# Sixteen-head attention on one core: diagonal blocks of four heads in one bank, output copies on ScalarE, the split of the maxima on GpSimd

## What is computed

```python
c_q = x @ W_dq
Q = (c_q @ W_uq).reshape(Bx, Sx, N_HEADS, D_K)      # 16 heads of 16
c_kv = x @ W_dkv
K = (c_kv @ W_uk).reshape(Bx, Sx, N_HEADS, D_K)
V = (c_kv @ W_uv).reshape(Bx, Sx, N_HEADS, D_K)
scores = jnp.einsum('bqhd,bkhd->bhqk', Q, K) / math.sqrt(D_K)
scores = jnp.where(causal, scores, -jnp.inf)
attn = jax.nn.softmax(scores, axis=-1)
out = jnp.einsum('bhqk,bkhd->bqhd', attn, V).reshape(Bx, Sx, N_HEADS * D_K)
return out @ W_o
```

## Time and profile before

| what | us |
|---|---|
| runs | 1255.91 median of 3 (1251.33 to 1259.59) |
| the profiled execution | 1263.3 span |
| attention steps in it | about 423 to 920 |
| engines over the span | TensorE 84%, VectorE 66%, ScalarE 53%, GpSimd 30% busy |

### The profile page before, as it was taken

The page is one execution under the profiler, slowest core; times in us unless marked ns, Lnnn a source line. Parts: engine busy times, 40 slices in busy tenths (PEclk is TensorE's granted clock), DMA queues, the critical chain, the costliest instruction groups (busy, mean ns, idle before and its releaser), DMA issues. The chain is left out here.

```text
span 1263.3 us, 22520 instructions
## 1 busy us (share of the span) xinstructions
PE 1066.7 (84%) x6988; PEld 642.3 (51%) x6988; DVE 829.9 (66%) x2536; ACT 666.1 (53%) x1668; POOL 384.3 (30%) x404
## 2 busy tenths in 40 slices
PE   3539999984988899999999999999859369999940
PEld 2328888872442244443444444444347258888840
DVE  6774444436867888888888888888037754444427
ACT  5605554542753376676777666667636315455520
POOL 6506777752002000000000000000048227777730
PEclk8559999995977699999999999999889759999985
DMA  9503333326756444444444444440057113333339
GB/s 301 186 9 93 101 105 105 102 84 216 201 200 142 59 60 61 61 61 60 61 61 60 60 61 61 61 60 11 10 189 239 58 38 94 104 102 104 105 118 331
DMA packets 109248, 132.53 MB, mean 105 GB/s; under 512 B 29968, under 2 KB 83664, under 8 KB 109136
## 3 DMA queue, kind: packets, MB, share of 16 engines
q1 hardware_dynamic: 91280, 89.65, 31.2%
q0 software_dynamic: 13632, 37.24, 9.3%
q10 hardware_dynamic: 4224, 4.19, 1.0%
HBM read 82.42 MB, written 48.23 MB: 103 GB/s over the span
## 5 line engine op out<-in xcount | busy, mean ns | idle before, releaser
L1415 ACT ACTIVATE stacks_rows_or_prob<-stacks_bank 128x512 f32<-128x512 f32 (+3 forms) x768 | 326.0, 494 | 144.1 <-PE stacks_bank L1347 118.9
L1429 DVE CUSTOM_DVE_ANT_0 stacks_bank<-stacks_bank,all_causal 128x128 f32<-128x128 f32 (+3 forms) x512 | 245.4, 504 | 33.7 <-PE stacks_bank L1318 30.2
L1432 DVE TENSOR_REDUCE t_maxp<-stacks_bank 128x1 f32<-128x512 f32 x256 | 175.5, 686 | 25.0 <-PE stacks_bank L1318 24.4
L1318 PE MATMUL stacks_bank<-stacks_kst,stacks_qst 96*128 96x512 bf16 (+2 forms) x528 | 160.3, 348 | 8.5 <-DVE t_maxp L1429 4.2
L1358 PE MATMUL stacks_bank<-stacks_rows_or_prob,stacks_turned_or_values 128*32 128x512 f32 (+3 forms) x1536 | 164.5, 500 | 3.0 <-ACT stacks_rows_or_prob L1415 1.1
L1344 PE MATMUL stacks_bank<-stacks_qst,stacks_kst 99*128 99x512 bf16 (+3 forms) x528 | 154.9, 335 | 2.5 <-ACT stacks_rows_or_prob L1415 1.9
L1296 POOL COPY stacks_turned_or_values<-stacks_values 128x512 f32<-128x512 f32 x16 | 9.8, 613 | 427.7 <-DMA stacks_kst<-qk_parts 286.5
L1318 PEld LDWEIGHTS stacks_bank<-stacks_kst,stacks_qst 96*128 96x128 bf16 x528 | 48.5, 98 | 126.9 <-DVE t_maxp L1429 66.6
L653 PE MATMUL be_psG<-b_w,be_xT 128*128 x426 | 112.8, 401 | 0.0
L653 PE MATMUL ae_psG<-a_w,ae_xT 128*128 x426 | 111.9, 398 | 0.0
L1347 PE MATMUL stacks_bank<-all_causal_t,all_ident_bf 128*128 128x128 bf16 x512 | 109.6, 221 | 0.0
(11 more groups left out here) (296 smaller groups left out, 1917.7 us busy)
## 6 DMA issues: line engine op xcount, KB each, us to landing
stacks_qst<-qk_parts SPq DMA_DIRECT2D x66, 128.0 KB, 4.9
stacks_kst<-qk_parts SPq DMA_DIRECT2D x66, 128.0 KB, 7.6
stacks_rows_or_prob<-y_rows SPq DMA_DIRECT2D x16, 512.0 KB, 6.1
s_yk<-y_rows SPq DMA_DIRECT2D x16, 512.0 KB, 9.4
stacks_parts_or_stacks<-qk_parts SPq DMA_DIRECT2D x60, 128.0 KB, 6.2
qk_parts<-stacks_parts_or_stacks SPq DMA_DIRECT2D x16, 384.0 KB, 2.6
qk_parts<-q_parts SPq DMA_DIRECT2D x16, 384.0 KB, 3.4
o_rows<-t_orow SPq DMA_DIRECT2D x32, 136.0 KB, 8.7
```

The lines of the kernel that those rows point to most:

```text
L1318: nc.tensor.matmul(psR[bank][:, 0:w], qst[slot][0:KROWS, h, i * P:(i + 1) * P], kst[slot][0:KROWS, h, k0:k0 + w], start=True, stop=True).t ...
L1415: nc.scalar.activation(prob[j % 2][:, h, a:(c + 1) * 512], psS[n % ST_BANKS][:, a - c * 512:512], ACT.Exp, scale=DK ** -0.5).then_inc(exp_ ...
L1429: ins = nc.vector.tensor_tensor_reduce(psR[bank][:, 0:w], psR[bank][:, 0:w], T.causal[:, 512 - w:512], 1.0, -BIG, ALU.add, ALU.max, maxp[: ...
L1432: ins = nc.vector.tensor_reduce(maxp[:, h, col:col + 1], psR[bank][:, 0:w], AX_X, ALU.max)
```

## The change

Three edits, all in the attention.

1. The turned scores of one key tile's diagonal block are taken out of the heads' units. For each j, one unit (j, c, None) of 4 x 128 columns holds the diagonal blocks of all four heads: one matmul with the mask repeated four times (512 columns) opens the bank, and four matmuls of 128 columns add the scores. The heads' own units are 128 columns narrower, and those of width 0 are gone. There are again 48 units. The planner knows the new units; its fixed cost of an exponential goes from 100 to 70 ns.
2. `copy_rows` moves from VectorE to ScalarE, behind the exponential that stands at the place of `turn_out` in the list. It has a semaphore of its own, `rows_copied`; who reuses that ring bank waits for it (`free_bank`).
3. Of `split_max`, negating stays on VectorE (`negate_max`); the other four instructions go to GpSimd. GpSimd's values copy is made two steps ahead, behind the split, where it was made in its own step.

The diff, cut to its core:

```diff
+def transposed_units():
+    units = []
+    for j in range(QT):
+        for c in range(j // QHALF, 2):
+            if c == j // QHALF:
+                units.append((j, c, None, HG * P))
+            w = (c + 1) * 512 - max(c * 512, (j + 1) * P)
+            units += [(j, c, h, w) for h in range(HG) if w > 0]
+    return units
...
-            _, j, c, h = st[n_st]
-            w = width(j, c)
-            t = start + (w + P * (max(c * 512, j * P) == j * P)) / 2.4
-            act = max(act, t + READER_LATENCY) + 100 + w * 0.833
+            j, c, h, w = st[n_st]
+            t = start + (w + (h is None) * w) / 2.4
+            act = max(act, t + READER_LATENCY) + 70 + w * 0.833
...
+        def split_max(g):
+            pool.wait_ge(drained, drained_to(max_at[g]))
+            wait(pool, m_loaded, g * (16 * PARTS))
+            nc.gpsimd.tensor_copy(mparts[:, 0], neg[:]).then_inc(split, 1)
+            pool.wait_ge(split, g * SPLIT + 1)
+            nc.gpsimd.tensor_tensor(mid[:], neg[:], mparts[:, 0], ALU.subtract).then_inc(split, 1)
+            pool.wait_ge(split, g * SPLIT + 2)
+            nc.gpsimd.tensor_copy(mparts[:, 1], mid[:]).then_inc(split, 1)
+            pool.wait_ge(split, g * SPLIT + 3)
+            nc.gpsimd.tensor_tensor(mparts[:, 2], mid[:], mparts[:, 1], ALU.subtract).then_inc(m_ready, 1)
+
+        def step(g, k, later, with_before):
+            if later:
+                split_max(g + 1)
+            if later > 1:
+                values_of(g + 2, (k + 2) % SLOTS)
...
-        def score_t(g, k, j, c, h):
-            n, a = n_st[j, c, h], max(c * 512, j * P)
-            ps = psS[n % ST_BANKS][:, a - c * 512:512]
-            wait(pe, exp_done, g * ST + n + 1 - ST_BANKS)
-            ins = nc.tensor.matmul(ps, kst[k][0:MROWS, h, j * P:(j + 1) * P], qst[k][0:MROWS, h, a:(c + 1) * 512],
-                                   start=True, stop=a > j * P)
-            if a == j * P:
-                ins = nc.tensor.matmul(ps[:, 0:P], T.ident_bf[:], T.causal_t[:], start=False, stop=True)
+        def score_t(g, k, n):
+            j, c, h, w = st_units[n]
+            ps, keys = psS[n % ST_BANKS], slice(j * P, (j + 1) * P)
+            wait(pe, st_read, g * ST + n + 1 - ST_BANKS)
+            if h is None:
+                nc.tensor.matmul(ps[:], T.ident_bf[:], bc(T.causal_t[:], 1, [P, HG, P]), start=True, stop=False)
+                for x in range(HG):
+                    ins = nc.tensor.matmul(ps[:, x * P:(x + 1) * P], kst[k][0:MROWS, x, keys], qst[k][0:MROWS, x, keys],
+                                           start=False, stop=(x == HG - 1))
+            else:
+                ins = nc.tensor.matmul(ps[:, 0:w], kst[k][0:MROWS, h, keys], qst[k][0:MROWS, h, (c + 1) * 512 - w:(c + 1) * 512],
+                                       start=True, stop=True)
             ins.then_inc(st_done, 1)
...
+        def copy_rows(g, c):
+            r = out_at(g, c) - 1
+            act.wait_ge(filled, r + 1)
+            wait(act, o_stored[c], g * 16)
+            nc.scalar.copy(orow[:, c], psR[r % RING_BANKS][:].rearrange("p (x w) -> p x w", w=VW)[:, :, 0:OW]).then_inc(rows_copied, 1)
...
+                if h is None:
+                    nc.scalar.activation(prob[j % 2][:, :, j * P:(j + 1) * P], psS[n % ST_BANKS][:].rearrange("p (h t) -> p h t", h=HG),
+                                         ACT.Exp, scale=DK ** -0.5).then_inc(st_read, 1)
...
+                for half in range(2):
+                    if n == turned[half]:
+                        copy_rows(g - 1, half)
...
-        def split_max(g, r, bank):
+        def negate_max(g, r, bank):
             dve.wait_ge(filled, r + 1)
-            wait(dve, m_loaded, g * (16 * PARTS))
+            wait(dve, m_ready, g)
             nc.vector.tensor_scalar(neg[:], psR[bank][0:MROW, 0:P], -1.0, None, ALU.mult).then_inc(drained, 1)
-            dve.wait_ge(drained, r + 1)
-            link(nc.vector.tensor_copy(mparts[:, 0], neg[:]), g, 2)
-            link(nc.vector.tensor_tensor(mid[:], neg[:], mparts[:, 0], ALU.subtract), g, 3)
-            link(nc.vector.tensor_copy(mparts[:, 1], mid[:]), g, 4)
-            nc.vector.tensor_tensor(mparts[:, 2], mid[:], mparts[:, 1], ALU.subtract).then_inc(m_ready, 1)
-
-        def copy_rows(g, c, r, bank):
-            dve.wait_ge(filled, r + 1)
-            wait(dve, o_stored[c], g * 16)
-            nc.vector.tensor_copy(orow[:, c], psR[bank][:].rearrange("p (x w) -> p x w", w=VW)[:, :, 0:OW]).then_inc(drained, 1)
```

More of the change, by code:

```diff
@@ L54 @@
 QT = S // P
+QHALF = QT // 2
 BIG = 3.0e38
@@ L1118, in score_units, with parts_of @@
     return units
+def transposed_units():
[7 more added lines that the diff above has]
+    return units
+def parts_of(units, j, c):
+    return [unit[:3] for unit in units if unit[:2] == (j, c)]
 def plan_step(units, later, with_before):
     width = lambda j, c: min((c + 1) * 512, S) - max(c * 512, j * P)
+    st = transposed_units()
     ring = [("s", u, 1) for u in range(AHEAD, len(units))] if later else []
@@ L1152, in plan_step @@
             _, j, c = pv[n_pv]
-            ready = max(exp_end.get((j, c, h), float("inf")) for h in range(HG))
+            ready = max(exp_end.get(key, float("inf")) for key in parts_of(st, j, c))
             can.append((max(t, ready), 0.0, "p"))
@@ L1175, in plan_step @@
             had_t += w
-            order.append(st[n_st])
+            order.append(("st", n_st))
             n_st += 1
@@ L1196, in programs_attention @@
     NS = len(units)
-    QHALF = QT // 2
     MROW = HG * QT
     n_pv = {(j, c): n for n, (j, c) in enumerate((j, c) for j in range(QT) for c in range(2) if j < QHALF * (c + 1))}
-    n_st = {(j, c, h): n * HG + h for (j, c), n in n_pv.items() for h in range(HG)}
+    st_units = transposed_units()
+    n_st = {unit[:3]: n for n, unit in enumerate(st_units)}
     PV, ST = len(n_pv), len(n_st)
@@ L1213, in programs_attention @@
     o_stored = [M.sem(f"o_stored{c}") for c in range(2)]
[L1214 to L1216 removed]
+    m_loaded, filled, drained, rows_copied, max_ready, m_ready, st_done, st_read, pv_done, o_copied, \
+        pool_done, joined, split = (
+            M.sem(n) for n in ("m_loaded", "filled", "drained", "rows_copied", "max_ready", "m_ready", "st_done", "st_read",
+                               "pv_done", "o_copied", "pool_done", "joined", "split"))
     RING0 = NS + 1 + AHEAD
@@ L1224, in programs_attention, with drained_to, free_bank @@
     assert RING % RING_BANKS == 0 and ST % ST_BANKS == 0
+    kinds = ["s"] * NS + ["m"] + ["s"] * AHEAD
+    for g in range(NG):
+        kinds += [x[0] for x in plans[min(2, NG - 1 - g), g > 0][1]]
+    kinds += ["o"] * 2
+    max_at = [r for r, kind in enumerate(kinds) if kind == "m"]
+    copied_by_act = list(itertools.accumulate(kind == "o" for kind in kinds))
+    def drained_to(r):
+        return r + 1 - copied_by_act[r]
+    def free_bank(pe, r):
+        before = r - RING_BANKS
+        if before >= 0 and kinds[before] == "o":
+            pe.wait_ge(rows_copied, copied_by_act[before])
+        elif before >= 0:
+            pe.wait_ge(drained, drained_to(before))
     def steps(step):
@@ L1290, in gpsimd, with values_of @@
         first = Q.pool_chain
-        def step(g, k, later, with_before):
+        def values_of(g, k):
             wait(pool, loaded[k], ((g - k) // SLOTS) * (16 * N_LOADS) + 16 * N_LOADS)
@@ L1297, in step @@
                                              rows.rearrange("p j (h w) -> p j h w", w=DK)))
-            if g == 0:
-                for s in range(1, SLOTS):
-                    blank(s)
-                pool.wait_ge(Q.v_ready, 2 * Q.CH)
-                for stored in Q.parts_stored:
-                    pool.wait_ge(stored, (Q.CH // 2) * (16 * Q.NU))
-                first.link(nc.gpsimd.memset(kst[SLOTS - 1][KROWS:MROWS, :, :], 1.0))
         def blank(s):
@@ L1312, in gpsimd @@
         pool.wait_ge(Q.v_ready, Q.CH)
+        values_of(0, 0)
+        for s in range(1, SLOTS):
+            blank(s)
+        pool.wait_ge(Q.v_ready, 2 * Q.CH)
+        for stored in Q.parts_stored:
+            pool.wait_ge(stored, (Q.CH // 2) * (16 * Q.NU))
+        first.link(nc.gpsimd.memset(kst[SLOTS - 1][KROWS:MROWS, :, :], 1.0))
+        split_max(0)
+        values_of(1, 1)
         steps(step)(pool)
@@ new lines, in step @@
+        def step(g, k, later, with_before):
+            order = plans[later, with_before][0]
+            turned = [sum(x[0] == "st" for x in order[:order.index(("o", c))]) if with_before else None for c in range(2)]
+            for n, (j, c, h, w) in enumerate(st_units):
+                if n == n_st[parts_of(st_units, j, c)[0]]:
+                    if j > 1:
+                        act.wait_ge(pv_done, g * PV + n_pv[j - 2, c] + 1)
+                    else:
+                        wait(act, pv_done, (g - 1) * PV + n_pv[j + QHALF * (c + 1) - 2, c] + 1)
+                act.wait_ge(st_done, g * ST + n + 1)
+                if h is None:
```

(13 more changed lines are left out.)

45 lines of the change are left out of this document (14 added, 31 removed).

## The result

| | before | after |
|---|---|---|
| median of 20 runs each, us | 1257.32 (1249.22 to 1264.19) | 1266.5 (1258.05 to 1278.82) |
| profiled execution, span | 1263.3 | 1266.4 |
| step 1's start to step 14's, 13 full steps | 401.55 | 411.28 |

The ratio of times is 1.0074, 95% interval 1.0052 to 1.0096: slower by 0.74%, inside the one per cent that I had called the same. The forecast was 1264.

What follows compares the result with a forecast made beforehand. TensorE's work before M plus the longer of work and chain behind it was taken as the bound; +0.44 and +0.07 a step, with late and edge steps, made +8.4 us, forecast 1264, range 1252 to 1282.

Steps and rivals of the forecast that it cites:

- order and merged pair, to M: TensorE ahead of M: 1,536 more columns add 0.64 us, adjacent PV blocks save 0.20; net +0.44 a step.
- M: Moment in each attention step when TensorE turns the next step's maxima; forecast about 25.4 us after the step's start.
- split on GpSimd, negate's end to last split: Four split instructions on GpSimd behind M: 1.74 us against 1.13 on VectorE, +0.61.
- landing, from M: Arrival of the DMAs of the maxima, needed before TensorE's next step: M + 5.21 us before, 0.61 later after.
- next step, from M: TensorE's resume at the step boundary: M + 5.87 us against 5.80, +0.07, with the landing deciding.
- step 14: Attention step that already hangs on the chain, 2.88 us idle: +0.2 of order and +0.6, +0.8 us.
- step 0: Entry and first attention step: VectorE earlier, landing later, work moved ahead of M mostly given back; together -0.6 us.
- rival A: VectorE's queue paces the part ahead of M, so relieving it gains 20 us: 1236; chance 0.12.
- the last exponential: Behind M, TensorE's last PV waits for ScalarE: 0.52 us for 0.21 of columns; this stall was to go.
- Rival B: GpSimd's split near its high end, +1.5 us, so +1.4 a full step: about +22, 1278; chance 0.17.
- Late landings: Three of 13 full steps waited for late maxima DMAs; there the whole +0.61 shows, not 0.07: +1.6 us.
- rival C: TensorE's idle 1.0 to 1.5 us each step makes its clock fall: +30 us, 1286; chance 0.06.

Runs made afterwards that it cites:

- d_split_only: The kernel before with only the split of the maxima moved to GpSimd; time ratio to the kernel before 1.0040, period 30.79 us.
- g_copies_dve: The changed kernel with only the output copies back on VectorE; time ratio to the kernel before 1.0106, period 31.35 us.
- e_banks_only: The changed kernel with split and output copies both back on VectorE, leaving diagonal banks and their order; ratio to the kernel before 1.0055, period 31.27 us.
- c_split_dve: The changed kernel with only the split of the maxima back on VectorE; time ratio to the kernel before 1.0078, period 31.34 us.
- h_longer_chain: The changed kernel with one of GpSimd's casts in the split made twice; time ratio to the kernel before 1.0224, period 31.75 us.

## Why the prediction was right, and where it was not

Step by step, the changed kernel against the working:

| step | forecast | measured |
|---|---|---|
| order and merged pair, to M | 24.92 + 0.44 | 25.52 (+0.60) |
| split on GpSimd, negate's end to last split | 1.74 | 1.75 |
| landing, from M | 5.82 | 5.84 |
| next step, from M | 5.87 | 5.89 |
| what decides there | landing, about 1 us idle | landing, 0.72 idle |
| full step | +0.51 | +0.69 |
| 13 full steps, late ones included | +8.2 | +9.7 |
| step 14 | +0.8 | +0.85 |
| step 0 | -0.6 | -0.8 |
| step 15 | 0 | +0.25 |
| total | +8.4 | +10.0 by these steps; +9.2 by the medians |

**The bound.** TensorE is full ahead of M and VectorE isn't the pace there: right. VectorE was given back 1.65 us a step and no shorter step came of it (rival A, 1236, fell). The clearest sign is d_split_only: VectorE has 1.0 us less to do in each step and M stands at 24.92 as before. Behind M the working named one stall of TensorE, the last exponential, and took the waits for VectorE as covered by the chain; they made about 0.5 of before's 5.80, as d_split_only shows.

**The split's cost.** Two casts of 0.28, two subtractions of 0.42, three links of 0.08 and 0.12 to be woken. Rival B, GpSimd at its dear end, fell. The row's line and fixed part gave 0.41 to 0.46 for the subtraction, so reading a small operation from the size rows worked. The Trainium skill, page "GPSIMD Engine Reference", section "Elementwise — side-by-side cycle accounting", would have made it an estimated 0.55; the trace shows 0.42 against 0.28 on VectorE, 1.5 times and not 1.96, at 128 elements a row. Its warning against the move was right in sign: the chain did grow, by 0.62 (1.75 against 1.13). The low end of the working, with its own terms, is +0.37 and not +0.3.

**What the sum missed.** The step "1,536 columns, 0.64 us, move ahead of M ... Net +0.44" was under-sized by 0.16. The copies of 272 columns measured 392 ns each, not "about 0.3", and cost 0.06 to 0.07 a step, inside the bound 0 to 0.3 of which I took 0. That leaves 0.09 (g_copies_dve, 24.92 to 25.45), which no run here gives to one instruction; small waits and gaps ahead of M are 0.07 more there than in before. The 0.20 for the merged pair was right: it is what the sum of shortest times falls by, 28.6 to 28.4.

**A right total with compensating parts.** The working put the order at +0.44 ahead of M and let its return behind M vanish under the longer chain. Read so, banks without the split should have returned 0.54 at M + 5.26, for -0.10 in all; the run shows +0.55, with the resume at M + 5.41. The failed step is "TensorE's last score unit also needs the bank of the fourth before it, which VectorE has read at about M + 4.4". In the changed kernel the last unit started at M + 4.78 and TensorE was idle from M + 5.17, not from M + 4.7, so the idle time was 0.72; the landing was still the binding wait, and it did no harm to the total there. With the split on VectorE the wait for VectorE binds at the boundary, as the releaser in e_banks_only and c_split_dve says, and VectorE carries its backlog into the next step's start (0.4 us ahead of M). I took VectorE for covered on both sides of M; it is covered ahead of M only if it comes out of the boundary without a queue, as the steps behind the late landings of e_banks_only show (25.45 against 25.86). So if one asks what each edit costs, my answer was wrong for the banks and their order, by 0.65 us a step, and for the split beside them (+0.07 in place of +0.61). The two errors have opposite signs and nearly cancel, so that the total held is in part luck: in the combination the landing hides VectorE's lateness.

**Late landings.** "+1.6: in the three late steps the whole +0.61 shows" was over-sized. There were two, 0.64 and 1.00 late and exposed in full, where before lost 1.18, 0.12 and 0.84 to its three, 2.14 in all. With the clock that the second one cost, 1.37, the net is +0.87. Part of that +0.87 is rival C in one step, which the working had put among the rivals alone.

**The clock.** A chance of 0.06 for C was too assured. The changed kernel idles 0.72, and 0.35 more turned 7 of 13 steps slow. The forecast held because my estimate of "1.0 to 1.5 us of idle TensorE" was too high, not because that much would have been harmless; had it been right, C was likely.

## What to carry to other kernels

When work is moved across a point at which a round trip starts (here the turn of the maxima, its split and its DMA), ask what covers the trip afterwards: here a list alone cost 0.57 us a step, and the split and the copies 0.07 each. Cost each edit with the others undone as well as in the combination: in my working the split looked dear and the banks free only because each was judged beside the other. Look at who reads the banks that the moved work needs next; here VectorE's reads, and not only the round trip, set what a list cost. A wait of under 1 us can stand beside a step for nothing more than itself, but measure how far it is from costing the clock, because the next 0.35 us was paid more than twice over here.

## What I had not expected of the hardware

- The clock fell for waits that recur, of mostly 1.07 us, in 7 of 13 steps (3.4 us at 1.2 GHz, 1.3 to 1.5 us lost each time), while the kernel before had a single one of 1.12 without a fall. Single waits don't sort by length either: 1.70 in g_copies_dve (step 5), 1.36 in after (step 5) and 1.27 in e_banks_only (step 12) kept the clock; 1.25 in c_split_dve (step 12), 1.29 and 1.39 in d_split_only, 1.72 in after and 2.46 in g_copies_dve lost it. What decides between them is open.
- Landings are late at the same steps, 5 and 12 (near 570 and 790 us), in 9 of the 14 profiles (the others have theirs at steps 4, 5, 10, 11 or 12): from M, 5.21 becomes 6.9 and 6.6 in before, 5.84 becomes 6.5 and 6.8 in after, 6.19 becomes 6.6 and 7.4 in h_longer_chain. In step 12 of after the second issue took 1.34 us and not 0.59, and landed 2.7 us after its start and not 1.9. What the queue meets there wasn't tried.
- Writing an exponential's 512 columns in four strided pieces cost nothing: 603 against 609 ns.
